# Three reorderings around the first layer norm's slices in a gated cross-attention block: ScalarE's copies, one slice's statistics, and the factor loads

## The reference, cut to what matters

```python
x = x + tanh(g_xattn) * attention(layernorm(x), ctx, ctx, Wq, Wk, Wv, Wd)   # 32 query heads, 8 key/value heads, causal over 256 rows
x = x + tanh(g_ffn)   * ffn(layernorm(x))                                    # silu(gate) * up, then down
# every ffn weight is w * (su @ sv): an elementwise product with a rank-4 factor
# x, ctx: 32 x 64 x 512 in float32 (2048 rows of 512)
```

## Time and profile before

| | |
|---|---|
| time, median of 3 runs | 1370.74 us (1370.12 to 1371.98) |
| the profiled execution | 1370.94 us, its span 1369.1 us |
| TensorE busy in the span | 1356.6 us (99%), granted clock 1.0 |
| VectorE, ScalarE, GpSimd busy | 959.8, 561.1, 954.4 us |
| the quads | from 54.38 to 497.9 us |

### The profile page before, as it was taken

One profiled execution on the slowest core, in us unless ns is written; L12 is line 12 of the kernel. 1 busy time (PEld: TensorE's weight loads), 2 busy tenths in 40 slices (PEclk: granted clock), 3 DMA queues, 4 the chain that ended last, 5 costly groups with the idle time before them and its releaser, 6 DMA issues.

```text
span 1369.1 us, 21420 instructions
## 1 busy us (share of the span) xinstructions
PE 1356.6 (99%) x7770; PEld 1112.6 (81%) x7770; DVE 959.8 (70%) x1465; ACT 561.1 (41%) x950; POOL 954.4 (70%) x883
## 2 busy tenths in 40 slices
PE   8999999999999999999999999999999999999998
PEld 8988788888888878778787877788888888888887
DVE  6388677665565677666667877774789888766776
ACT  5455555555444523232223334232344434334333
POOL 5599989999887946445454666573787787666664
PEclk9999999999999999999999999999999999999999
DMA  8386787777978866454445556621322331311121
GB/s 294 123 264 220 238 265 237 270 250 234 335 256 294 283 232 224 154 165 129 153 162 150 185 154 200 200 65 45 78 56 68 92 85 47 123 54 47 47 69 70
DMA packets 158057, 226.47 MB, mean 165 GB/s; under 512 B 43264, under 2 KB 89600, under 8 KB 155904
## 3 DMA queue, kind: packets, MB, share of 16 engines
q1 hardware_dynamic: 157952, 225.09, 51.0%
HBM read 155.32 MB, written 69.73 MB: 164 GB/s over the span
## 4 chain that ended last, share of the span: by engine, by line
PE 83%; POOL 10%; DVE 2%; issue 2%; ACT 1%; DMA 1%; SPq 0%; DVEq 0%; ACTq 0%; POOLq 0%
PE bank L616 65%; POOL wa_lo L1676 5%; PE bank L888 4%; PE bank L890 4%; PE bank L766 4%; PE bank L889 4%; PE bank L742 3%; POOL ws L1664 1%; POOL ws L1667 1%; POOL ws L1665 1%; POOL ws L1669 1%; DVE xc L1274 1%; PE bank L659 0%; DMA er_raw<-in_sf_r 0%; POOL xb L1645 0%
## 5 line engine op out<-in xcount | busy, mean ns | idle before, releaser
L616 PE MATMUL bank<-xc,wa_hi 128*128 128x512 f32 x896 | 277.7, 391 | 0.8 <-ACT s L1012 0.8
L616 PE MATMUL bank<-wd_hi,o_hi 128*128 128x512 f32 x512 | 202.9, 396 | 0.5 <-issue 0.5
L616 PE MATMUL bank<-wd_lo,o_hi 128*128 128x512 f32 x512 | 199.5, 390 | 0.0
L616 PE MATMUL bank<-wd_hi,o_lo 128*128 128x512 f32 x512 | 199.2, 389 | 0.0
L616 PEld LDWEIGHTS bank<-xc,wa_hi 128*128 128x128 f32 x896 | 167.3, 188 | 38.1 <-ACT s L1012 2.5
L616 PE MATMUL bank<-xc,wa_lo 128*128 128x512 f32 x448 | 174.5, 390 | 0.0
L1063 ACT ACTIVATE o_hi<-bank 128x512 fp32r<-128x512 f32 x128 | 69.5, 595 | 228.3 <-PE bank L766 151.1
L1477 DVE SCALAR_TENSOR_TENSOR X<-bank,tg,X 128x512 f32<-128x512 f32 x221 | 154.4, 741 | 0.0
L616 PE MATMUL bank<-x_hi,wf_hi 128*128 128x512 f32 x392 | 152.6, 389 | 0.1
L616 PE MATMUL bank<-x_hi,wf_lo 128*128 128x512 f32 x392 | 152.5, 389 | 0.0
L616 PE MATMUL bank<-x_lo,wf_hi 128*128 128x512 f32 x364 | 141.6, 389 | 0.0
(11 more groups left out here) (175 smaller groups left out, 3157.0 us busy)
## 6 DMA issues: line engine op xcount, KB each, us to landing
q_scratch<-q_st SPq DMA_DIRECT2D x32, 1024.0 KB, 4.8
q_sb<-q_scratch SPq DMA_DIRECT2D x64, 512.0 KB, 4.8
w_raw<-in_wq SPq DMA_DIRECT2D x32, 512.0 KB, 4.1
wd_raw<-in_wd SPq DMA_DIRECT2D x16, 1024.0 KB, 4.8
f_raw<-ffn_eff_scratch SPq DMA_DIRECT2D x28, 512.0 KB, 3.7
er_raw<-in_sf_r SPq DMA_DIRECT2D x42, 256.0 KB, 4.3
e_raw<-in_wf SPq DMA_DIRECT2D x42, 256.0 KB, 5.4
ffn_eff_scratch<-e_eff SPq DMA_DIRECT2D x42, 256.0 KB, 5.2
```

What stands on the lines that cost most here:

```text
L616: last = pe.matmul(to, a, b, start=(start and n == 0), stop=(stop and n == 3 * len(pairs) - 1), skip_group_check=onto)
```

## The change

It moves instructions on three engines and adds none.

1. ScalarE, in column quads from q = 8 on (9, 13, 17, 21, 25): `left_hi(w + 1)` comes behind the copy `s1` instead of ahead of it. In a column quad that directly follows an `X_SPLIT` quad (of these only q = 9), `x_columns` comes behind the result copy `c11` instead of ahead of it.
2. VectorE: the statistics of the second slice (m = 1) were at the end of quad 3; they are now in quad 4 behind `t1`, as for all other slices.
3. SyncE: in all quads that load factors, but the one where they change buffers (`E_MOVE`, m + 1 = 7), `load_lr(m + 1)` comes right behind `store_q(q - 1)`, ahead of `store_e`, `load_e` and the load of the next context chunk.

```diff
             if q:
                 store_q(q - 1)
+            if q in E_AT and m + 1 < NP and m + 1 != E_MOVE:
+                load_lr(m + 1)
             if m:
                 store_e(m - 1)
                 load_e(m)
             if q + 6 < len(LOADS):
                 load_c(q + 6)
-            if q in E_AT and m + 1 < NP:
+            if q in E_AT and m + 1 == E_MOVE:
                 load_lr(m + 1)
...
         def quad(q):
             w = q - NV
-            if -1 <= w < NW - 1 and q < NQ - 1:
+            copy_first = q in COLUMNS and w >= 0
+            copied_first = copy_first and q - 1 in X_SPLIT
+            if -1 <= w < NW - 1 and q < NQ - 1 and not copy_first:
                 left_hi(w + 1)
             a.wait_ge(p_p[1], q + 1)
             if q:
                 a.wait_ge(v_t2, q)
             a.activation(s1[:, :], bank[0][:, :], ACT.Copy).then_inc(a_s1, 1)
+            if copy_first:
+                left_hi(w + 1)
...
-            if q in COLUMNS:
+            if q in COLUMNS and not copied_first:
                 x_columns(COLUMNS[q])
...
             a.activation(result(q, 0, 0), split(q, bank[0][:, :]), ACT.Copy).then_inc(a_c11, 1)
+            if copied_first:
+                x_columns(COLUMNS[q])
...
             if q in APPLY:
-                if q - 1 not in X_SPLIT:
-                    stats1(APPLY[q])
+                stats1(APPLY[q])
                 ln_moments(APPLY[q])
...
-            if q in STATS and q in X_SPLIT:
-                stats1(STATS[q])
```

## The result

| | before | changed |
|---|---|---|
| time, median | 1370.34 us (1368.42 to 1371.98, 10 runs) | 1373.09 us (1372.28 to 1377.02, 10 runs) |
| ratio | | 1.003, 95% interval 1.0021 to 1.0039 |
| span of the profiled execution | 1369.1 us | 1371.5 us |
| quads, start of the first matmul of quad 0 to start of the last of quad 43 | 443.37 us | 445.45 us |

What follows compares the result with a forecast made beforehand. GpSimd's round of 40.59 us was taken as the bound; its shifts of -0.9 and four times +0.48, with -0.3 to -0.4 in quad 30, ended at +0.6: 1371.4 us, range 1367.9 to 1373.3 (own range 1370.7 to 1372.6).

Steps and rivals of the forecast that it cites:

- What bounds the quads: GpSimd's round of 40.59 us for four quads, against 39.84 that TensorE needs, was the loop to watch.
- a meeting: VectorE's `lr_lo` starts 0.01 us ahead of GpSimd's `shift` and blocks the shared port: `shift` takes 0.73 instead of 0.20.
- Statistics after `t1`: Quad 4: the 0.74 us stall goes, up to -0.9 with its tail; a wait for VectorE's sum leaves -0.3.
- Result copy first: Quad 10: the 0.99 + 0.1 us go, shift -1.4; a wait for GpSimd leaves -0.35 at quad 11, then -0.5.
- `s1` first: Quads 13, 17, 21, 25: GpSimd's wait grows 0.48 us each; TensorE's loss of 0.7 goes in 13, 21, 25.
- the sum by GpSimd's side: Shifts of GpSimd's round at quads 13, 17, 21, 25: -0.4, +0.05, +0.53, +1.0 us; TensorE follows, end +0.6.
- Quad 13: -0.9 + 0.48 = -0.4: GpSimd's round at quad 13: -0.9 us by the sooner factors, +0.48 by the later first hi part.
- Quad 17: +0.05: GpSimd's round at quad 17: the next 0.48 us of later hi part brings its shift to +0.05.
- Ties fall the other way: Rival, 0.19: in quads 20 and 24 `shift` starts just before `lr_lo` and takes 0.20; two times -0.53 us: 1370.4.
- GpSimd has slack: Rival, 0.16: margin at quad 24 not used up, or port conflicts melt away; all stalls go, 1366.9 us, half 1368.9.
- Late FFN weight: Rival, 0.09: `load_e` behind the wait of `load_lr` lands late, in a loop; 0.1 us in 30 quads: 1374.4.
- The factors don't come sooner: Rival, 0.06: the wait for `lr_lo` holds `load_lr` where it was; without -0.9 and -0.35, 1372.7 us.

Runs made afterwards that it cites:

- e11: The kernel before with only the second slice's statistics moved behind `t1` in quad 4; 1369.03 us, ratio 0.9993.
- e12: The kernel before with only ScalarE's result copy moved ahead of the column copies in quad 9; 1370.57 us, ratio 1.0001.
- e2: The kernel before with only `s1` moved ahead of the hi parts in quads 9, 13, 17, 21 and 25; 1372.82 us, ratio 1.0023.
- the square above: Changed kernel, e5, e9 and e10: GpSimd's wait behind `shift` 2.64 or 2.15 us, `shift` held up or not; quads +2.11, -0.18, +0.19, -1.96 against before.
- e9: The changed kernel with the first of three hi parts ahead of `s1` again in the column quads, the other two behind it; 1371.46 us, ratio 1.0013.
- e5: The changed kernel, with VectorE waiting for `shift` before the factors' lo parts in quads 12, 16, 20 and 24; 1371.33 us, ratio 1.0016.
- e6: The changed kernel with all hi parts ahead of `s1` again, and VectorE waiting for `shift` as in e5; 1369.03 us, ratio 0.9994.
- e7: The kernel before with only VectorE's wait for `shift` as in e5; 1369.24 us, ratio 0.9993.
- e10: The changed kernel with the split hi parts of e9 and VectorE's wait of e5; 1370.51 us, ratio 1.0001.

## Why the prediction was wrong

- **What bounds the quads**: right as far as it went. GpSimd's round is the bound from quad 13 to 28, and TensorE's stalls, 0.74 in quad 4, 0.99 in quad 10 and 0.7 in each of three column quads, were removed without any gain. But the 0.7 of quads 21 and 25 were themselves the price of a meeting; the prediction noted that quad 17 did not lose and did not ask why.
- **Statistics after `t1`**: the stall went (quad 5 starts 0.92 sooner) and -0.3 was taken as what stays. The wait for VectorE's sum in quad 5 came, as the row above has it (`v_st`), and took all of it back: in e11, which has this part alone, quad 8 stands at -0.05. Mis-sized by 0.25, with no effect on the end. (The changed kernel's quad 8 stands at +0.18 and its quad 9 at +0.35; so do those of e12, +0.19 and +0.37, which changed nothing up to there, so this is not the change's doing.)
- **Result copy first**: quad 9 is 0.99 shorter, as forecast, so that quad 10 stands at -0.63 (forecast -1.4), quad 11 at -0.35 (forecast -0.35, a hit by luck since it started from elsewhere), quad 12 at -0.11 (forecast -0.5). In e2 the move of `s1` alone shortens quad 9 by as much. In quads 11 and 12 TensorE starts 0.14 and 0.21 behind the end of GpSimd's lo part, so that is the limit, and not the 0.34 read off; the margin at quad 24 was 0.13 and not 0.04. The mechanism, a wait for GpSimd in its place, is right.
- **`s1` first**: the gap grew by 0.48 as forecast, and the square above gives it 1.8 to 1.9 us in four quads, as the forecast had it (4 x 0.48).
- **The step that failed is the sum by GpSimd's side**, in two of its terms. "Quad 13: -0.9 + 0.48 = -0.4" came out as +0.37, against quad 0's start: GpSimd's `shift` began 0.27 later and took 0.53 longer, and the gap was 0.43 shorter than in that quad before (3.07, by the late factors, to 2.64). The -0.9 was reckoned on ScalarE's side alone: the end of GpSimd's `shift` was taken as fixed at 188.14, and it came at 189.12. "Quad 17: +0.05", another +0.45, came out as +1.21: the round there was 39.8 us before, with no meeting, and became 41.02 with one, 0.48 + 0.53 and 0.2, nearly all of it from the first meeting ahead of it. The forecast had read one round, 40.59 from quad 17 to 21, and used it for all. The two later rounds grew by 0.43 and 0.46, nearly the 0.48 of the forecast. Together +2.46 at quad 25 where the forecast had +1.0. Quad 30 gave 0.36 back (forecast 0.3 to 0.4), and +2.08 are left at the end.
- **The prediction had the lever in its hand and pointed it one way.** *Ties fall the other way* priced the meeting at 0.53 and asked only whether quads 20 and 24 would lose it. That quads 12 and 16 would gain it, the same +1.06 on the other side, was not a rival. With it the forecast would have been 1372.5 or more.
- *GpSimd has slack*: no; TensorE waits for GpSimd in every round, 0.6 at quads 15, 19, 23 and 27. *Late FFN weight*: real, but in quad 42 alone, 1.9 to 2.7 us in four of the eight profiled executions with the factors sooner; the changed kernel's own has none of it. *The factors don't come sooner*: no; ScalarE's wait for them in quad 12 is gone.

What stays open is what settles the order at the first meeting, where hundredths of a microsecond decide. In the profiled executions the meeting of `shift` came in none, two, three or four of the quads, in kernels that are alike up to tenths of a microsecond. A reading that fits: both engines' instructions wait for each other's ends, so that they take only certain distances; with a meeting GpSimd's round is longer than what TensorE needs (40.55 against 39.85 at the same gap), GpSimd sets the pace and the distance stays; without one TensorE sets the pace, and `er` stays 0.8 behind. Then the longer gap of the changed kernel, which makes GpSimd the pace setter by itself, would hold the first state: in the three profiled executions with a gap of 2.6 or more and no added wait, all twelve places met. That is argued and not tested by itself. Nor was one kernel profiled several times to see its state change; the kernel before, whose profiled execution switched at quad 20, may fall into either, and that would be part of its 1367.8 to 1373.5.

## What to carry to other kernels

Where a helper engine paces the bound engine, list that engine's whole round before and after, each round on its own, and ask of every short instruction in it what it would take if another engine's longer one started just ahead; a price that is known to exist in two of four places belongs into the range in both directions. Moving a copy that the bound engine waits for ahead of one that the pacing engine waits for trades a visible wait for an invisible one; giving the pacing engine its one input first and only then the copy (e9) left the gap at 2.15 and the column quads at 10.66 to 10.69 us, though here it did not make the kernel faster than before. And where a wait labelled "issue" ends right behind another engine's last write of the operand, look whether it is a wait for that engine.

## What the runs showed of the hardware

- A GpSimd operation of 128x2 takes 0.20 us alone and 0.73 when a 32x512 VectorE operation with two SBUF inputs has started 0.01 to 0.02 us before it: 0.53 us for an instruction that has next to nothing to do, and on the path each time. With VectorE held back by a semaphore `shift` took 0.20 in all sixteen places of e5, e6, e7 and e10; in nine of them the wait is what held VectorE back (it started 0.54 behind `shift`), in seven it came later by itself.
- The same between longer operations: a VectorE sum of 128x512 with two SBUF inputs takes 0.69 us and a GpSimd sum of 128x256 0.73; where they meet, the one that started second takes up to 1.27, whichever it is (quads 16 and 20 of the kernel before).
- TensorE's matmul can start as little as 0.14 us behind the end of the GpSimd instruction that it waits for (quad 11), and 0.22 at quad 19; both times it had been waiting.
- The same 256 KB load, issued in the same quad (42) of the eight kernels with the factors sooner, took from 3.5 to 7.8 us from issue to landing in their profiled executions.
